# A convolution, router and low-rank experts on one core: tiles 2 and 3 in float32 with shared blocks, the first biases behind the sums, and another order of the early steps

## Chip, cores and metric

The kernel runs on one core of one Trainium2 chip. The metric is the device time of one execution in microseconds (us); the time of a kernel is the median of its runs.

## What is computed

The input x has 128 sequences of 32 channels and 512 positions. Cut to what matters:

```python
def reference(x, cond, conv_b, conv_w, cond_w, base_W, base_b, router_W, router_b, A, B, expert_map):
    c = conv1d(x, conv_w, taps=9, pad=4, groups=4) + (cond @ cond_w.T)[:, :, None] + conv_b[None, :, None]
    base = c @ base_W.T + base_b                          # 512 -> 512, along the positions
    probs = softmax(c @ router_W.T + router_b)            # 15 routes
    p, i = top_k(probs, 8)
    w = sum of p over the routes that expert_map sends to each of 8 experts
    h = (c @ A) * w                                       # 8 experts of rank 16: 128 columns
    return x + base + 2.0 * (h @ B)                       # all float32
```

## The kernel before, in words

A row is one sequence and channel. The 4096 rows are 32 tiles of 128; tile t holds group t % 4 of the convolution's channels for 16 sequences. The 512 positions are cut into 32 blocks of 16, so that a block of 8 channels by 16 positions fills the 128 partitions, and the convolution is a matmul with banded weights over blocks: an output block needs its own input block and a neighbour.

**Convolution.** The first four tiles (START = 4) are done in plain float32 by `conv_first` (L557 to L566): two matmuls a tile, 128x128 by 512 columns each (own block, neighbour), from `x_in`. From tile 4 on, `conv` (L568 to L593) works with less arithmetic: blocks are taken in pairs, the sum of weights meets one block (`S_SUM`), the own weights meet a difference of blocks (`S_OWN`), 256 columns each, and once for each two tiles a third product (`S_QUARTERS`, from `edges`) corrects both tiles' reaching halves in `edge_ps`. Each of these is three matmuls in the faster number format (float32r, written as high and low parts: high by high, low by high, high by low).

**Linear part.** The conditioned rows are transposed (`turn`, L861) into y and split into `y_hi` (ScalarE, `y_high` L396) and `y_lo` (GpSimd, `y_low` L501). `linear` (L598) multiplies them with `wide_hi` and `wide_lo` in four runs of the contraction: the front bank (128 columns of A, 16 of the router, half of the base: 400 columns) and the next bank (256 columns). `turn_hw` (L625) transposes the weighted h on TensorE, `up` (L637) adds h @ B onto the same banks in six matmuls of 256 columns.

**Order on TensorE** for tile t from 2 on (L757 to L770): wait for `out_added` of tile t - 2 (its bank is used again) and for `y_hi`; front bank of tile t (12 matmuls); `turn_hw` of tile t - 1; next bank, runs 0 and 1 (6); `up` of tile t - 1 (6); next bank, runs 2 and 3 (6); `conv` of tile t + 3 (6, or 9 when t + 3 is even). Tiles 0 and 1 have `first_step` (L678) and `second_step` (L712) of their own.

**Order on VectorE**, written out in `step` (L920 to L968): `condition` of tile t + 2 (L792: two adds of 256 columns, the second waiting for the first, then the 64-partition add from `edge_ps` at L809, which waits for the second), `turn` of t + 2 at once, `hw_low` (L873) of t - 1, `choose` (L819, adds the router's bias, starts when the front bank is done), `difference` of t + 4 (L813), `best` (L825), `add_out` of t - 1 (L776, adds the bank to the x rows), `mark` (L829), `weigh` (L834: five small operations, the last writes `hw`).

**ScalarE** (L430): `y_high`, `hw_high` (L403), `exponentials` (L365), `terms_high` (L381), `edge_high`, `odd_up` (L374, copies half of the terms into PSUM for `difference`). **GpSimd** (L519): `y_low`, `bias_rows` (L478, adds the base bias onto the x rows in `xr`, before `add_out` for every tile), `terms_low` (L483), `edge` or `edge_low`; in the start `conv_low` (L471) splits the convolution's weights. **SyncE** issues nearly all transfers, in the order of L273 to L300 and then of `step` (L302). Every operation signals a semaphore and each engine works its list in order: what waits holds up all behind it on that engine.

## Time and profile before

| | |
|---|---|
| median of 3 runs | 184.4 us (184.03 to 184.5) |
| the profiled execution | 184.55 us, its span 182.7 us |
| TensorE busy | 178.6 us, 98% of the span |
| VectorE busy | 150.9 us, 83% |
| GpSimd busy | 140.1 us, 77% |
| ScalarE busy | 81.3 us, 44% |
| granted TensorE clock | full (2.4 GHz) in all 40 slices |
| DMA | 32.01 MB, 175 GB/s over the span |
| chain that ended last | TensorE 97% |

The profiled execution's own time is 1.85 us more than its span, and 0.15 us above the median. TensorE's busy share counts pipelined matmuls, so it is read beside the chain and the waits.

### The profile page before, as it was taken

Reading aid. Unit: us, or ns where it says so; the run is one execution under the profiler, and the core shown is the slowest. Engines: PE = TensorE matmul, PEld = TensorE weight load, DVE = VectorE, ACT = ScalarE, POOL = GpSimd, SP = SyncE. Lnnn points to the kernel's source line nnn. Section 1 sums busy time; section 2 is a strip of 40 time slices with the busy share of each in tenths; the row PEclk is TensorE's granted clock in tenths of the full one; section 3 lists DMA queues with packets and bytes.
Section 4 is the critical chain, followed back from the end, with each engine's and each line's share of the span. In section 5 each row is a group of like instructions: output and inputs, shape, how many; then the busy total and the mean of one; then the engine's idle time right before and its main releaser. Section 6 shows DMA issues by size and latency. Waiting matters only on the chain.

```text
span 182.7 us, 3929 instructions
## 1 busy us (share of the span) xinstructions
PE 178.6 (98%) x1236; PEld 171.3 (94%) x1236; DVE 150.9 (83%) x509; ACT 81.3 (44%) x247; POOL 140.1 (77%) x139
## 2 busy tenths in 40 slices
PE   7999999999999999999999999999999999999993
PEld 3786999999999999999999999999999999999992
DVE  0597899888888889888888988889898889978673
ACT  3657834354544334454433445453344444422320
POOL 2127999999888898888889888888988887885610
PEclk9999999999999999999999999999999999999999
DMA  6999750766475653546475454745635721333304
GB/s 159 362 382 346 251 174 24 218 183 234 155 233 174 185 181 105 170 165 230 134 215 178 140 164 158 229 178 194 182 124 163 256 83 58 98 115 115 118 0 172
DMA packets 17876, 32.01 MB, mean 175 GB/s; under 512 B 1984, under 2 KB 3136, under 8 KB 17856
## 3 DMA queue, kind: packets, MB, share of 16 engines
q1 hardware_dynamic: 17424, 31.40, 52.7%
q10 hardware_dynamic: 432, 0.36, 0.6%
q8 instruction: 10, 0.16, 0.4%
q14 instruction: 10, 0.08, 0.2%
HBM read 23.36 MB, written 8.39 MB: 174 GB/s over the span
## 4 chain that ended last, share of the span: by engine, by line
PE 97%; DVE 1%; issue 0%; POOL 0%; DVEq 0%; POOLq 0%
PE wide_ps L605 61%; PE wide_ps L647 12%; PE conv_banks L591 11%; PE edge_bank L591 3%; PE conv_banks L605 2%; PE odd_bank L634 2%; PE wide_ps L553 1%; PE conv_banks L662 1%; PE conv_banks L564 1%; PE conv_banks L562 1%; DVE xr L978 1%; PE edge_bank L620 0%; PE conv_banks L647 0%; PE edge_bank L634 0%; POOL zeros L462 0%
## 5 line engine op out<-in xcount | busy, mean ns | idle before, releaser
L605 PE MATMUL wide_ps<-wide_hi,y_hi 128*128 128x400 f32 (+1 forms) x248 | 65.7, 325 | 0.0
L605 PE MATMUL wide_ps<-wide_lo,y_hi 128*128 128x400 f32 (+1 forms) x248 | 62.6, 313 | 0.0
L605 PE MATMUL wide_ps<-wide_hi,y_lo 128*128 128x400 f32 (+1 forms) x248 | 62.5, 312 | 0.0
L485 POOL TENSOR_TENSOR terms_lo<-terms,terms_hi 128x512 fp32r<-128x512 f32 x28 | 36.3, 1296 | 18.1 <-ACT terms_hi L385 18.0
L605 PEld LDWEIGHTS wide_ps<-wide_lo,y_hi 128*128 128x128 f32 x248 | 45.9, 188 | 0.2 <-DVE wide_lo L883 0.2
L605 PEld LDWEIGHTS wide_ps<-wide_hi,y_hi 128*128 128x128 f32 x248 | 43.9, 188 | 2.2 <-ACT y_hi L400 0.6
L605 PEld LDWEIGHTS wide_ps<-wide_hi,y_lo 128*128 128x128 f32 x248 | 45.8, 188 | 0.1
L503 POOL TENSOR_TENSOR y_lo<-y,y_hi 128x512 fp32r<-128x512 f32 x31 | 40.2, 1297 | 6.0 <-ACT y_hi L400 6.0
L480 POOL TENSOR_TENSOR xr<-xr,base_b_sb 128x512 f32<-128x512 f32 x32 | 41.5, 1300 | 0.0
L407 ACT ACTIVATE hw_hi<-odd_bank 128x128 fp32r<-128x128 f32 x31 | 8.6, 278 | 53.7 <-PE odd_bank L634 53.6
L780 DVE TENSOR_TENSOR xr<-wide_ps,xr 128x512 f32<-128x512 f32 x30 | 20.7, 691 | 5.2 <-PE wide_ps L647 3.6
L868 DVE STREAM_TRANSPOSE y<-y_rows 128x512 f32<-128x512 f32 x32 | 22.8, 711 | 1.1
L400 ACT ACTIVATE y_hi<-y 128x512 fp32r<-128x512 f32 x31 | 19.4, 624 | 3.8 <-DVE y L868 2.8
L367 ACT ACTIVATE minus_best<-top 128x1 f32<-128x1 f32 x32 | 6.5, 202 | 32.0 <-DVE top L827 32.0
L385 ACT ACTIVATE terms_hi<-terms 128x512 fp32r<-128x512 f32 x28 | 17.3, 618 | 0.5 <-DVE terms L816 0.5
L591 PE MATMUL conv_banks<-terms_hi,conv_hi 128*128 128x256 f32 x56 | 15.7, 280 | 0.0
L591 PE MATMUL conv_banks<-terms_hi,conv_lo 128*128 128x256 f32 x56 | 15.7, 280 | 0.0
L591 PE MATMUL conv_banks<-terms_lo,conv_hi 128*128 128x256 f32 x56 | 15.6, 278 | 0.0
L854 DVE SCALAR_TENSOR_TENSOR hw<-wide_ps,inv,expert_w 128x128 f32<-128x128 f32 x31 | 10.9, 351 | 4.9 <-DVE expert_w L848 0.5
L816 DVE TENSOR_TENSOR terms<-terms,odd_bank 128x256 f32<-128x256 f32 x28 | 11.7, 420 | 1.7 <-ACT odd_bank L379 0.8
L647 PE MATMUL wide_ps<-up_hi,hw_lo 128*128 128x256 f32 x62 | 12.7, 284 | 0.0
L806 DVE TENSOR_TENSOR y_rows<-conv_banks,y_rows 128x256 f32<-128x256 f32 x28 | 11.9, 425 | 1.0
(90 smaller groups left out, 308.9 us busy)
## 6 DMA issues: line engine op xcount, KB each, us to landing
xr<-x_rows SPq DMA_DIRECT2D x32, 256.0 KB, 3.6
out<-xr SPq DMA_DIRECT2D x31, 256.0 KB, 3.2
terms<-x_units SPq DMA_DIRECT2D x28, 256.0 KB, 2.9
edges<-x_edges SPq DMA_DIRECT2D x14, 256.0 KB, 3.1
wide_sb<-wide_w SPq DMA_DIRECT2D x4, 328.0 KB, 4.6
x_in<-x_first SPq DMA_DIRECT2D x3, 264.0 KB, 4.4
weights_sb<-conv_w SPq DMA_DIRECT2D x2, 192.0 KB, 5.3
x_in<-x_first SPq DMA_DIRECT2D x2, 132.0 KB, 2.8
```

Of the source, the lines that this page charges most:

```text
L385: nc.scalar.activation(terms_hi[i % 2][:, :, :, :], terms[i][:, :, :, :], ACT.Copy)\
L400: nc.scalar.activation(y_hi[k % 2][:, :, :], y[k % 2][:, :, :], ACT.Copy)\
L480: nc.gpsimd.tensor_tensor(xr[k][:, :], xr[k][:, :], base_b_sb[:, :], ALU.add)\
L485: nc.gpsimd.tensor_tensor(terms_lo[i % 2][:, :, :, :], terms[i][:, :, :, :], terms_hi[i % 2][:, :, :, :].bitcast(F32), ALU.subtract)\
L503: nc.gpsimd.tensor_tensor(y_lo[k % 2][:, :, :], y[k % 2][:, :, :], y_hi[k % 2][:, :, :].bitcast(F32), ALU.subtract)\
L591: mm = nc.tensor.matmul(sums, w[:, j, :], a[:, :, :], start=w is conv_hi and a is hi, stop=a is lo)
L605: mm = nc.tensor.matmul(sums_of(t, k)[:, b, 0:columns[1] - columns[0]], a[k % 2][:, r, :], w[:, r, columns[0]:columns[1]], start=r == 0 an ...
L647: mm = nc.tensor.matmul(sums_of(t, k)[:, b, first:first + HALF], a[k % 2][:, :], w[:, b * HALF:(b + 1) * HALF], start=False, stop=True, sk ...
L780: nc.vector.tensor_tensor(rows, linear_sums(t, k), rows, ALU.add)\
L806: nc.vector.tensor_tensor(rows[:, :, other, :], conv_ps[:, h, 1, :, :], rows[:, :, shared, :], ALU.add).then_inc(own_ready, 1)
L816: nc.vector.tensor_tensor(terms[i][:, 0, :, :], terms[i][:, 0, :, :], odd_ps, ALU.subtract).then_inc(differences_ready, 1)
L868: nc.vector.transpose(y[k % 2][:, :, :].rearrange("p r (n o) -> p n r o", n=Q), y_rows[k % 2][:, :, :, :].rearrange("p n a k -> p n (a k)"))\
```

## The change

Tiles 2 and 3 leave `conv_first` and are done with paired blocks too, but in plain float32 (`conv_whole`: two matmuls of 256 columns, and for tile 2 a third that serves both). Their differences of blocks are new operations: two on GpSimd before `conv_low(1)`, which wait for all of VectorE's `wide_low`, and one on VectorE before `weigh(0)`. Loads change with them; the weights have 12 blocks in place of 14, and the base bias comes as a full 128-row array in place of a broadcast of one row.

The bias of tiles 0 to 3 is added behind `add_out` instead of ahead of it; `bias_rows` of tiles 1 to 4 moves to later places of GpSimd's list. The stores of these tiles wait for it.

`condition` keeps its two adds; the third is `reach`, which comes after `best`. In every step from 4 on VectorE does `choose`, `best`, `reach`, `add_out`, `mark`, `difference`, `weigh` and then `turn`; steps 0 to 3 are written out. ScalarE does `y_high` behind `hw_high` (steps 2 and 3: behind `exponentials`). On TensorE the blocks of tile 4 are done in `second_step`, its edges in step 2.

```diff
+W_OWN, W_REACH, W_SUM, W_QUARTERS = (1, 2, 4, 7), (0, 3), (9, 10, 5, 8), (11, 6)
+W_ALL = 12
...
+first_terms = [sb(f"first_terms{i}", [P, 2, Q, MK]) for i in range(START - FIRST)]
+first_edges = sb("first_edges", [P, 2, Q, MK])
...
     load_conv(2)
-    load_x(2)
-    sync.wait_ge(wide_in[0], 16)
+    load_first_terms(0)
+    sync.wait_ge(wide_in[1], 16)
+    sync.dma_start(first_edges[:, :, :, :], x_edges[0]).then_inc(first_edges_in, 16)
+    load_conv(4)
+    sync.wait_ge(wide_in[2], 16)
     load_conv(3)
-    load_x(3)
-    sync.wait_ge(wide_in[2], 16)
+    load_first_terms(1)
+    sync.wait_ge(wide_in[3], 16)
     load_terms(START, 0)
     load_edges(START // 2, 0)
     sync.dma_start(up_sb[:, :], up_w).then_inc(up_in, 16)
-    sync.dma_start(base_b_sb[:, :], base_b.partition_broadcast(P)).then_inc(base_b_in, 16)
+    sync.dma_start(base_b_sb[:, :], base_b).then_inc(base_b_in, 16)
     sync.dma_start(xr[0][:, :], x_rows[0]).then_inc(xr_loaded[0], 16)
     load_terms(START + 1, 1)
-    sync.wait_ge(x_loaded[3], 16)
+    sync.wait_ge(first_terms_in[1], 16)
     sync.dma_start(xr[1][:, :], x_rows[1]).then_inc(xr_loaded[1], 16)
     load_terms(START + 2, 2)
     load_edges(START // 2 + 1, 1)
-    load_conv(4)
     load_terms(START + 3, 3)
...
-            sync.wait_ge(out_added, t - 1 if t < TILES else t)
+            if up_to_tile(t, POST + 1):
+                sync.wait_ge(xr_biased, t - 1)
+            else:
+                sync.wait_ge(out_added, t - 1 if t < TILES else t)
...
     y_high(1, 1, 2)
+    exponentials(0, 0)
     odd_up(START, 0)
-    exponentials(0, 0)
-    terms_high(START, 0)
     act.wait_ge(up_in, 16)
     nc.scalar.activation(up_hi[:, :], up_sb[:, :], ACT.Copy, scale=LORA_SCALE)\
         .then_inc(up_hi_ready, 1)
     nc.scalar.activation(up_scaled[:, :], up_sb[:, :], ACT.Copy, scale=LORA_SCALE)\
         .then_inc(up_scaled_ready, 1)
+    terms_high(START, 0)
     edge_high(START // 2, 0)
...
-        if up_to_tile(t, TILES - 2):
+        if from_tile(t, TILES - 3) and up_to_tile(t, TILES - 2):
             y_high(t + 1, k + 1)
...
         hw_high(t - 1, k - 1)
+        if t == 1:
+            act.wait_ge(hw_lo_ready, 1)
+            odd_up(START + 1, 1)
+        if t == 1 or from_tile(t, START) and up_to_tile(t, TILES - 4):
+            y_high(t + 1, k + 1)
         if up_to_tile(t, TILES - 2):
             exponentials(t, k)
-        if t == 1:
-            act.wait_ge(hw_lo_ready, 1)
-            odd_up(START + 1, 1)
+        if t == 2 or t == 3:
+            y_high(t + 1, k + 1)
...
+        if from_tile(t, POST):
+            pool.wait_ge(xr_loaded[k], (t - k) * 4 + 16)
+        else:
+            pool.wait_ge(out_added, t + 1)
         nc.gpsimd.tensor_tensor(xr[k][:, :], xr[k][:, :], base_b_sb[:, :], ALU.add)\
...
     conv_low(0)
+    pool.wait_ge(wide_lo_ready, RUNS)
+    pool.wait_ge(first_terms_in[0], 16)
+    nc.gpsimd.tensor_tensor(first_terms[0][:, 0, :, :], first_terms[0][:, 0, :, :],
+                            first_terms[0][:, 1, :, :], ALU.subtract)\
+        .then_inc(first_difference[0], 1)
+    pool.wait_ge(first_edges_in, 16)
+    nc.gpsimd.tensor_tensor(first_edges[:, 0, :, :], first_edges[:, 0, :, :],
+                            first_edges[:, 1, :, :], ALU.subtract)\
+        .then_inc(first_edge_ready, 1)
     conv_low(1)
     y_low(1, 1, 2)
...
         if t == 0:
+            up_low()
             terms_low(t + 4, k)
-            up_low()
             edge_low(p + 2, k // 2)
+            y_low(t + 2, k + 2)
             pool.wait_ge(base_b_in, 16)
-            bias_rows(t, k)
-            y_low(t + 2, k + 2)
+            bias_rows(0, 0)
             return
         if t == 1:
             terms_low(t + 4, k)
-            bias_rows(t, k)
             edge(p + 3, 1 - k // 2)
             y_low(t + 2, k + 2)
+            return
+        if t == 2:
+            terms_low(t + 4, k)
             conv_low(2)
+            edge_low(p + 2, k // 2)
             conv_low(3)
+            bias_rows(1, 1)
             return
-        if from_tile(t, 3) and up_to_tile(t, TILES - 2):
+        if up_to_tile(t, TILES - 2):
             y_low(t + 1, k + 1)
-        if up_to_tile(t, TILES - 1):
+        if from_tile(t, START + 1) and up_to_tile(t, TILES - 1):
             bias_rows(t, k)
...
+        if t == 3:
+            bias_rows(2, 2)
+        if t == 4:
+            bias_rows(3, 3)
+            bias_rows(4, 0)
...
+    def conv_blocks(t, g):
...
+    def products(sums, j, hi, lo):
+        for w, a in ((conv_hi, hi), (conv_lo, hi), (conv_hi, lo)):
+            mm = nc.tensor.matmul(sums, w[:, j, :], a[:, :, :],
+                                  start=w is conv_hi and a is hi, stop=a is lo)
+        return mm
...
+    def conv_blocks(t, g):
         h = g % 2
         pe.wait_ge(terms_lo_ready, t - START + 1)
...
+        pe.wait_ge(y_rows_ready, t - 1)
         if t < 2 * START and h == 0:
             pe.wait_ge(conv_lo_ready, 2 + g // 2 * 2)
...
+        products(conv_ps[:, h, 0, :, :], S_SUM[g], terms_hi[h][:, 1], terms_lo[h][:, 1])
+        return products(conv_ps[:, h, 1, :, :], S_OWN[g], terms_hi[h][:, 0],
+                        terms_lo[h][:, 0])
+    def conv_edges(t, g, p):
+        pe.wait_ge(y_rows_ready, t)
+        pe.wait_ge(edge_lo_ready, p - START // 2 + 1)
+        return products(edge_ps, S_QUARTERS[g // 2], edge_hi, edge_lo)
+    def conv(t, g, p):
+        mm = conv_blocks(t, g)
+        if g % 2 == 0:
+            mm = conv_edges(t, g, p)
         mm.then_inc(conv_done, 1)
...
             pe.wait_ge(odd_ready, 1)
+            pe.wait_ge(differences_ready, 1)
...
-    def conv_later(t):
+    def conv_whole(t):
+        i, h = t - FIRST, t % 2
         pe.wait_ge(y_rows_ready, t - 1)
-        pe.wait_ge(conv_w_in[2], 16)
-        pe.wait_ge(x_loaded[t], 16)
-        conv_first(t)
+        pe.wait_ge(conv_w_in[2 + i], 16)
+        pe.wait_ge(first_terms_in[i], 16)
+        nc.tensor.matmul(conv_ps[:, h, 0, :, :], conv_sb[:, W_SUM[t], :],
+                         first_terms[i][:, 1, :, :], start=True, stop=True)
+        pe.wait_ge(first_difference[i], 1)
+        mm = nc.tensor.matmul(conv_ps[:, h, 1, :, :], conv_sb[:, W_OWN[t], :],
+                              first_terms[i][:, 0, :, :], start=True, stop=True)
+        if h == 0:
+            pe.wait_ge(cond_biased, GROUPS)
+            pe.wait_ge(first_edge_ready, 1)
+            mm = nc.tensor.matmul(edge_ps, conv_sb[:, W_QUARTERS[t // 2], :],
+                                  first_edges[:, 0, :, :], start=True, stop=True)
+        mm.then_inc(conv_done, 1)
...
         y_rest(1)
+        w_rest(0)
         high(2)
         y_rest(2)
-        w_rest(0)
+        w_rest(1)
         high(3)
         linear(0, 0, (3,), products=(Y_REST,), last=(RUNS - 1, W_REST))
-        w_rest(1)
         w_rest(2)
...
-        conv_later(2)
+        conv_whole(2)
     def second_step():
         runs = range(RUNS)
         pe.wait_ge(y_hi_ready, 2)
         linear(1, 1, runs, (FRONT_BANK,), (HIGH,))
         linear(1, 1, runs, (FRONT_BANK,), (W_REST,))
+        conv_whole(3)
         pe.wait_ge(y_lo_ready, 2)
         linear(1, 1, runs, (FRONT_BANK,), (Y_REST,)).then_inc(front_done, 1)
-        conv_later(3)
         turn_hw(0, 0)
-        linear(1, 1, runs[:3], (NEXT_BANK,))
+        linear(1, 1, runs[:2], (NEXT_BANK,))
         up(0, 0)
-        linear(1, 1, runs[3:], (NEXT_BANK,)).then_inc(linear_done, 1)
+        linear(1, 1, runs[2:], (NEXT_BANK,)).then_inc(linear_done, 1)
+        conv_blocks(START, 0)
...
+            if t == 2:
+                conv_edges(START, 0, START // 2).then_inc(conv_done, 1)
             up(t - 1, k - 1)
...
-        if from_tile(t, 1) and up_to_tile(t, TILES - 4):
+        if from_tile(t, 2) and up_to_tile(t, TILES - 4):
             conv(t + 3, (k + 3) % GROUPS, p + 2)
...
-        dve.wait_ge(xr_biased, t + 1)
+        if from_tile(t, POST):
+            dve.wait_ge(xr_biased, t + 1)
+        else:
+            dve.wait_ge(xr_loaded[k], 16)
...
         dve.wait_ge(conv_done, t + 1)
         c = cond_sb[:, g, bass.ds(q * Q, Q)]
         nc.vector.tensor_tensor(rows[:, :, shared, :], conv_ps[:, h, 0, :, :],
                                 c.unsqueeze(2).to_broadcast([P, Q, MK]), ALU.add)\
             .then_inc(common_ready, 1)
-        dve.wait_ge(common_ready, t - START + 1)
+        dve.wait_ge(common_ready, t - FIRST + 1)
         nc.vector.tensor_tensor(rows[:, :, other, :], conv_ps[:, h, 1, :, :],
                                 rows[:, :, shared, :], ALU.add).then_inc(own_ready, 1)
-        dve.wait_ge(own_ready, t - START + 1)
...
+    def reach(t, g):
...
+        h = g % 2
+        shared = 1 - h
+        rows = y_rows[h]
+        reached = slice(EDGE, P) if h == 0 else slice(0, EDGE)
...
+        dve.wait_ge(own_ready, t - FIRST + 1)
         nc.vector.tensor_tensor(rows[reached, :, shared, :], edge_ps[reached],
                                 rows[reached, :, shared, :], ALU.add)\
             .then_inc(y_rows_ready, 1)
...
     best(0, 0)
-    difference(START, 0)
     dve.wait_ge(top_ready, 1)
     mark(0, 0)
+    dve.wait_ge(first_terms_in[1], 16)
+    nc.vector.tensor_tensor(first_terms[1][:, 0, :, :], first_terms[1][:, 0, :, :],
+                            first_terms[1][:, 1, :, :], ALU.subtract)\
+        .then_inc(first_difference[1], 1)
     dve.wait_ge(is_expert_ready, 1)
     weigh(0, 0)
+    difference(START, 0)
     dve.wait_ge(cond_biased, GROUPS)
...
         if t == 0:
-            condition_first(2)
+            condition(2, 2, 0)
+            hw_low(0, 0)
+            reach(2, 2)
             turn(2, 2)
             choose(1, 1)
             dve.wait_ge(logits_ready, 2)
             best(1, 1)
+            return
+        if t == 1:
+            add_out(0, 0)
             dve.wait_ge(top_ready, 2)
             mark(1, 1)
-            condition_first(3)
-            hw_low(0, 0)
+            difference(START + 1, 1)
+            weigh(1, 1)
+            condition(3, 3, 0)
+            reach(3, 3)
             return
-        if t == 1:
+        if t == 2:
+            hw_low(1, 1)
+            choose(2, 2)
+            dve.wait_ge(logits_ready, 3)
+            best(2, 2)
             turn(3, 3)
-            difference(START + 1, 1)
-            add_out(0, 0)
-            weigh(1, 1)
+            add_out(1, 1)
+            dve.wait_ge(top_ready, 3)
+            mark(2, 2)
+            difference(START + 2, 2)
+            weigh(2, 2)
+            condition(4, 0, 1)
+            reach(4, 0)
+            return
+        if t == 3:
+            condition(5, 1, 1)
+            hw_low(2, 2)
+            choose(3, 3)
+            dve.wait_ge(logits_ready, 4)
+            best(3, 3)
+            turn(4, 0)
+            reach(5, 1)
+            add_out(2, 2)
+            dve.wait_ge(top_ready, 4)
+            mark(3, 3)
+            difference(START + 3, 3)
+            weigh(3, 3)
+            turn(5, 1)
             return
         if up_to_tile(t, TILES - 3):
             condition(t + 2, (k + 2) % GROUPS, q + (k + 2) // GROUPS)
-            turn(t + 2, k + 2)
-            hw_low(t - 1, k - 1)
-        elif t == TILES - 2:
+        if up_to_tile(t, TILES - 2):
             hw_low(t - 1, k - 1)
...
-        if up_to_tile(t, TILES - 2):
-            choose(t, k)
-            dve.wait_ge(logits_ready, t + 1)
-            if up_to_tile(t, TILES - 5):
-                difference(t + 4, k)
-            best(t, k)
-            dve.wait_ge(top_ready, t + 1)
-            if up_to_tile(t, TILES - 3):
-                add_out(t - 1, (k - 1) % UNROLL)
-            mark(t, k)
-            weigh(t, k)
+        choose(t, k)
+        dve.wait_ge(logits_ready, t + 1)
+        best(t, k)
+        if up_to_tile(t, TILES - 3):
+            reach(t + 2, (k + 2) % GROUPS)
+            if from_tile(t, TILES - 4):
+                turn(t + 2, k + 2)
+        dve.wait_ge(top_ready, t + 1)
+        if up_to_tile(t, TILES - 3):
+            add_out(t - 1, (k - 1) % UNROLL)
+        mark(t, k)
+        if up_to_tile(t, TILES - 5):
+            difference(t + 4, k)
+        weigh(t, k)
+        if up_to_tile(t, TILES - 5):
+            turn(t + 2, k + 2)
```

In `first_step` the product with `wide_lo` of runs 0 and 1 is done one place earlier each. The last four steps keep `turn` behind `reach`, ahead of `add_out`.

## Rows read from the trace of the kernel before

**Rows 1.** The page: span and the engines' busy time and share

```profile
span 182.7 us, 3929 instructions
...
PE 178.6 (98%) x1236; PEld 171.3 (94%) x1236; DVE 150.9 (83%) x509; ACT 81.3 (44%) x247; POOL 140.1 (77%) x139
```

**Rows 2.** Waits of TensorE (PE) in the whole span: total, times, longest

```profile
PE wide_ps L553 <- POOL zeros L462: 1.0, 1, 1.0
```

**Rows 3.** The chain that ended last, in order: start us, us, what

```profile
6.23 0.43 PE conv_banks L662 x2
...
13.02 0.86 PE conv_banks L562 x2
```

**Rows 4.** Timeline of TensorE's weight loads: start us, us, instruction, idle before

```profile
14.53 0.67 PEld L605 LDWEIGHTS wide_ps<-wide_hi,y_hi 128*128 128x128 f32 x4 [0.61 <-ACT y_hi L400]
```

**Rows 5.** Timeline of ScalarE (ACT): start us, us, instruction, idle before

```profile
13.85 0.63 ACT L400 ACTIVATE y_hi<-y 128x512 fp32r<-128x512 f32 x1 [1.90 <-DVE y L868]
...
35.11 0.28 ACT L407 ACTIVATE hw_hi<-odd_bank 128x128 fp32r<-128x128 f32 x1 [2.05 <-PE odd_bank L634]
```

**Rows 6.** Timeline of TensorE's matmuls, tiles 1, 2, 4, starts of 6 and 29

```profile
16.09 0.90 PE L605 MATMUL wide_ps<-wide_hi,y_lo 128*128 128x400 f32 x4
...
18.54 0.27 PE L634 MATMUL odd_bank<-ident,hw 128*128 128x128 f32 x1
...
21.85 0.97 PE L605 MATMUL wide_ps<-wide_hi,y_hi 128*128 128x400 f32 x4
...
32.57 0.88 PE L605 MATMUL wide_ps<-wide_hi,y_hi 128*128 128x400 f32 x4
...
34.74 0.27 PE L634 MATMUL odd_bank<-ident,hw 128*128 128x128 f32 x1
...
35.56 0.40 PE L647 MATMUL wide_ps<-up_hi,hw_hi 128*128 128x256 f32 x2
...
43.19 0.90 PE L605 MATMUL wide_ps<-wide_hi,y_hi 128*128 128x400 f32 x4
...
165.24 0.89 PE L605 MATMUL wide_ps<-wide_hi,y_hi 128*128 128x400 f32 x4
```

**Rows 7.** Timeline of VectorE (DVE), start and the steps of tiles 4 and 5

```profile
9.31 3.09 DVE L883 TENSOR_TENSOR wide_lo<-wide_sb,wide_hi 128x656 fp32r<-128x656 f32 x4
...
21.08 0.69 DVE L780 TENSOR_TENSOR xr<-wide_ps,xr 128x512 f32<-128x512 f32 x1 [0.53 <-POOL xr L480]
...
35.83 0.42 DVE L816 TENSOR_TENSOR terms<-terms,odd_bank 128x256 f32<-128x256 f32 x1
36.17 0.17 DVE L827 MAX8 top<-logits 128x8 f32<-128x15 f32 x1
36.57 0.69 DVE L780 TENSOR_TENSOR xr<-wide_ps,xr 128x512 f32<-128x512 f32 x1 [0.24 <-PE wide_ps L647]
...
37.53 0.18 DVE L838 SCALAR_TENSOR_TENSOR wide_ps<-wide_ps,exps 128x15 f32<-128x15 f32 x1
...
38.75 0.41 DVE L802 TENSOR_TENSOR y_rows<-conv_banks,cond_sb 128x256 f32<-128x256 f32 x1
39.20 0.42 DVE L806 TENSOR_TENSOR y_rows<-conv_banks,y_rows 128x256 f32<-128x256 f32 x1
39.66 0.42 DVE L809 TENSOR_TENSOR y_rows<-edge_bank,y_rows 64x256 f32<-64x256 f32 x1
```

**Rows 8.** Timeline of GpSimd (POOL) in steps 4 and 5

```profile
37.01 1.30 POOL L480 TENSOR_TENSOR xr<-xr,base_b_sb 128x512 f32<-128x512 f32 x1
38.27 1.30 POOL L485 TENSOR_TENSOR terms_lo<-terms,terms_hi 128x512 fp32r<-128x512 f32 x1
39.50 0.75 POOL L497 TENSOR_TENSOR edge_lo<-edges,edge_hi 128x256 fp32r<-128x256 f32 x1
40.20 1.31 POOL L503 TENSOR_TENSOR y_lo<-y,y_hi 128x512 fp32r<-128x512 f32 x1
```

68 lines of the change are left out of this document (28 added, 40 removed).

## The prediction

> **What bounds the kernel.** I read the page first: TensorE ends the chain, and VectorE and GpSimd are at 83% and 77% of a span of 182.7 us [rows 1]. Then the waits of TensorE: it waited once, 1.0 us at the very start [rows 2]. So every microsecond behind it is matmul time, and only two things change the end: less matmul work, or a stall of TensorE where there is none now. Then the chain in order, for prices, and last the timelines of the four engines between 9 and 44 us, to see how early each operand is ready. I write F(t) for the moment the front bank of tile t is done (start of the hw transpose); before, F(1) = 18.54, F(4) = 34.74 [rows 6].
>
> **TensorE's work.** A float32 matmul of 256 columns takes 0.43 us in the chain, one of 512 columns 0.86 [rows 3] (the chain splits each into two passes). Tiles 2 and 3 now cost 4 x 0.86 = 3.44 us, afterwards 3 + 2 matmuls of 256 columns, 5 x 0.43 = 2.15. That removes 1.29 us. The other moves on TensorE (blocks and edges of tile 4, the order of `first_step`) keep the count of matmuls; the last `wide_lo` still gates tile 0: VectorE has it at 9.31 + 3.09 = 12.40 [rows 7].
>
> **Tile 2's share is not cashed.** Tile 2's convolution starts at about 12.86 (the chain books it 0.16 later [rows 3]). Its third product waits for two GpSimd subtractions which wait for `wide_low`: 12.44 + 2 x 0.72 = 13.9, priced by the same form, 0.75 [rows 8]. It would be over at 14.35. But tile 1's front bank needs `y_hi`, which ScalarE finishes at 13.85 + 0.63 = 14.48 [rows 5], and TensorE's loads already sat idle for it until 14.53 [rows 4]. Nothing ahead of it on VectorE or ScalarE changes, so tile 1 starts at 14.53 again: 0.43 us of the 1.29 become a wait, and the two subtractions are hidden by that same wait (without it they cost 0.2). GpSimd's `y_lo` of tile 1 is now late (16.2), which is why tile 3's convolution stands ahead of it.
>
> **Tile 3's share is.** The low product of tile 1 started at 16.09 [rows 6]; now two matmuls (0.86) come first, then 0.73: F(1) = 17.69, 0.85 earlier than 18.54. hw of tile 0 is ready at about 16.4: its `exponentials` go ahead of `odd_up` on ScalarE (-0.30), the new subtraction on VectorE (0.34) hides behind them. Transfers: some 300 KB more come ahead of tile 4's terms, under 1 us; each new landing that I sum stays 0.7 us or more ahead of its user, and the base bias no longer is read as a broadcast.
>
> **VectorE gets more work.** Before, tiles 2 and 3 took one add of 512 columns each; now three adds of 256, some 0.65 us more per tile, and 0.34 for the subtraction: about 1.6 us in a stretch where it had no more than 0.53 us idle at one place [rows 7]. Against it stands the new order. An add that waits for the add ahead of it starts 0.45 behind it (38.75, 39.20, 39.66), while a free one of 0.42 is followed after 0.34 (35.83 to 36.17) [rows 7]. Taking `reach` and `turn` away from the adds they wait for, and putting `difference` between `mark` and `weigh`, frees 0.11 + 0.10 + 0.14 + 0.18 = 0.53 us a tile; VectorE's list falls from 5.12 to about 4.6 us, under TensorE's 5.1 and 5.5 (two tiles from 32.57 to 43.19 are 10.62 [rows 6]). Followed step by step with these prices: `add_out(0)` ends at 20.57, tile 2 starts at 20.64 (was 21.85, with 0.35 us of tile 4's edges ahead of it, now behind: gain 0.86); the edges of tile 4 need `reach(3)`, 23.6, and come at 23.7; `hw_low(2)`, behind four adds and a fifth, is 0.1 us late for `up(2)`; tile 4 starts at 31.82 (was 32.57) and F(4) = 34.0. The gain there is 0.74.
>
> **GpSimd is late once, at tile 6.** The bias of tile 4 is still added ahead of `add_out(4)`, and step 4 puts it last: `y_low(5)`, `terms_low(8)`, `edge_low`, bias of tile 3, bias of tile 4. `terms_low(8)` waits for `terms_hi(8)`, this for `difference(8)`, this for `add_out(3)`, which waits for `up(3)`: F(4) + 1.83 (36.57 against 34.74 [rows 6, 7]). From there: `add_out` and `mark` 0.78 (0.96 from 36.57 to 37.53 [rows 7], less the 0.18 in which `weigh` waits for `mark`, and `difference` will not), `difference` 0.42, `terms_hi` 0.62 (the form of `y_hi`, 0.63) [rows 5, 7] with 0.1 of handing over: F(4) + 3.77. GpSimd then needs 1.25 + 0.70 + 1.25 + 1.30 = 4.50 (37.01 to 38.27, 39.50 to 40.20 [rows 8]), and the bias is there at F(4) + 8.27; `add_out(4)` takes 0.69 [rows 7]: F(4) + 9.0. TensorE wants to start tile 6, on that bank, two tiles after tile 4: its own work from F(4) is 43.19 - 34.74 = 8.45 [rows 6]. So it stands still for about 0.6 us. Bounds: if `terms_low(8)` never waited (GpSimd is free 0.4 us before), 0.15; if GpSimd were late by one more bias, 1.8. I take 0.6, since every price in the sum has its own row. The stores of tiles 0 to 3 now wait for the late biases, and on SyncE the loads of rows and terms stand behind them; followed through, each is still issued over 6 us ahead of its user. Of the gain of 0.74 about 0.1 is left, with a weight load exposed after the stall.
>
> **The steady part.** From step 5 on the same operations are in another order. Counted from F(t): `hw_hi` is ready at 0.65 (35.11 + 0.28 against 34.74 [rows 5, 6]), `hw_low` ends at 0.92 and is wanted at 1.29; `add_out` 1.83 to 2.52, wanted at 2.95 or 3.3; `weigh` takes 1.22 (37.53 to 38.75 [rows 7]), hw is ready at 4.3 and wanted at 5.1 or 5.5; `y_hi` at 1.2 and GpSimd's `y_lo` at 2.6, both wanted over 1.5 us later. None is late; in the last steps, with `turn` ahead of `add_out`, the bank is free 0.04 us before it is wanted, so up to 0.1 may be lost. From tile 6 to tile 29 TensorE took 165.24 - 43.19 = 122.05 us, 11.5 pairs of 10.61 [rows 6], all alike, so at most small delays sit in each. VectorE will reach `hw_low` and hw a little sooner than now. I count 0.2 us over all tiles as gained, a guess between 0 and 0.5 (0.04 a pair).
>
> **Sum.** 1.29 removed; 0.43 waits for `y_hi`, 0.1 late `hw_low`, 0.65 at tile 6 with its load, 0.2 gained later: -0.3 us. On the profiled execution, span 182.7 and 184.55 in all, this is 184.25; its time stands 0.15 over the median of 184.4, so I give 184.1.
>
> **Rivals.** A difference of 0.3% of this time, 0.55 us, is about what a measurement can tell from none.
>
> A (mine, 0.52): 184.1; its own range is 183.7 to 184.5.
>
> B, GpSimd is in time at tile 6 and the 0.75 stays: 184.4 - 0.75 - 0.2 = 183.45. For it: the margin of all of step 4 hangs on one chain, and 0.15 is its lower bound. Against: `terms_hi` was what GpSimd waited for in the old order too, and the new one makes it later. A larger gain in the steady part has the same effect. 0.30.
>
> C, slower: VectorE's starts do not move closer. Then its list stays 5.12 us a tile, the 1.6 us of new work is not absorbed, and the place is `hw_low` of tiles 2 to 4: I get 30.5 for `hw_low(2)` against 29.7 wanted, `add_out(2)` 0.2 behind tile 4's start, then 0.3 more at `up(3)`, and tile 6 starts 0.7 us later than before: 184.4 + 0.7 = 185.1. It decides from the point where `hw_low` ends later than F(t) + 1.29. Against: the 0.34 and 0.45 us in [rows 7]. The page "VectorE: DVE Perf Modes" of the Trainium skill, section "The DRAIN you can't avoid", says that the next operation starts only when the pipeline is empty and that a semaphore between two operations costs nothing extra; by that C is what should come, and these rows differ from it. 0.10.
>
> D: the change gains nothing because a wait that I price at 0 (the edges of tile 4, `out_added` for tile 2, the last steps) takes the rest: 184.4 and up to 184.9. 0.08.
>
> **Numbers.** 184.1 us. Range 183.3 to 184.9: it takes in B and D and leaves out C. Faster by over 0.3%: B and the lower edge of A, 0.36. Within: 0.52. Slower by over 0.3%: C and a little of D, 0.12.
>
> **What would show it.** Right: one wait of TensorE near 42.5 us for VectorE's `add_out`, itself waiting for GpSimd's bias, 0.5 to 0.7 us; F(1) near 17.7 with tile 1 still started at 14.5 behind `y_hi`; tile 4 started near 31.8; VectorE with idle time in every step. Wrong: no wait of TensorE at tile 6 (B); an add and a `reach` or `hw_low` behind it 0.45 apart, or waits of `up` for `hw_lo` (C); tile 1 started before 14.4, which would cash tile 2's share as well; waits of TensorE behind 50 us.

## The result, and the profile after

The changed kernel takes 186.53 us (186.22 to 186.96, 6 runs); the kernel before, run beside it, 184.45 (184.03 to 185.3). The ratio is 1.010, 95% interval 1.0075 to 1.0126: slower by 1.4 to 2.3 us, outside the predicted range of 183.3 to 184.9. The profiled execution took 186.76 us with a span of 184.9. One of the twelve runs of e9 below took 998 us and is left out; no other run stands apart like this.

The page, span and engines, beside [rows 1]:

```profile
span 184.9 us, 3931 instructions
...
PE 179.8 (97%) x1238; PEld 172.2 (93%) x1238; DVE 146.9 (79%) x514; ACT 83.2 (45%) x247; POOL 141.4 (76%) x141
```

The waits of TensorE over the whole span, beside [rows 2]:

```profile
PE wide_ps L598 <- POOL zeros L485: 1.0, 1, 1.0
PE wide_ps L653 <- DVE xr L852: 0.5, 1, 0.5
PE wide_ps L699 <- DVE hw_lo L954: 0.3, 1, 0.3
```

Two waits are new and together 0.8 us; the kernel lost about 2. So the waits don't tell the loss. What does is the moment at which TensorE starts the front bank of each tile. The timeline of TensorE, beside [rows 6] (start us, us, instruction; the starts of tiles 0, 1, 2, 4, 6, 7, 24, 28 and 29, the transposes that follow the front banks of tiles 1 and 4, and the late product of `up(2)`):

```profile
9.26 0.57 PE L653 MATMUL wide_ps<-wide_hi,y_hi 128*128 128x400 f32 x2
...
15.07 0.99 PE L653 MATMUL wide_ps<-wide_hi,y_hi 128*128 128x400 f32 x4
...
18.22 0.27 PE L684 MATMUL odd_bank<-ident,hw 128*128 128x128 f32 x1
...
21.40 0.99 PE L653 MATMUL wide_ps<-wide_hi,y_hi 128*128 128x400 f32 x4
...
30.94 0.50 PE L699 MATMUL wide_ps<-up_hi,hw_lo 128*128 128x256 f32 x2 [0.30 <-DVE hw_lo L954]
...
33.05 0.34 PE L653 MATMUL wide_ps<-wide_hi,y_hi 128*128 128x400 f32 x1
...
35.24 0.27 PE L684 MATMUL odd_bank<-ident,hw 128*128 128x128 f32 x1
...
44.30 0.45 PE L653 MATMUL wide_ps<-wide_hi,y_hi 128*128 128x400 f32 x1 [0.45 <-DVE xr L852]
...
49.55 0.34 PE L653 MATMUL wide_ps<-wide_hi,y_hi 128*128 128x400 f32 x1
...
140.19 0.35 PE L653 MATMUL wide_ps<-wide_hi,y_hi 128*128 128x400 f32 x1
...
161.75 0.34 PE L653 MATMUL wide_ps<-wide_hi,y_hi 128*128 128x400 f32 x1
...
167.19 0.45 PE L653 MATMUL wide_ps<-wide_hi,y_hi 128*128 128x400 f32 x1
```

From such rows of every profile comes this table. Each column is a stretch between two of these starts, in us; "end" runs from tile 29 to the end of the span, "sum" from the front bank of tile 0 to the end of the span. The span is given to 0.1 us, so the last two columns are good to 0.05. The experiments below are in it already, since they are read by it.

| kernel | tile 0 at | 0 to 4 | 4 to 7 | 7 to 24 | 24 to 28 | 28 to 29 | end | sum |
|---|---|---|---|---|---|---|---|---|
| before | 8.72 | 23.85 | 15.73 | 90.43 | 21.37 | 5.14 | 17.46 | 173.98 |
| before (e9) | 8.51 | 23.81 | 15.75 | 90.42 | 21.38 | 5.12 | 17.51 | 173.99 |
| after | 9.26 | 23.79 | 16.50 | 90.64 | 21.56 | 5.44 | 17.71 | 175.64 |
| e1, bias early | 9.53 | 23.80 | 15.81 | 90.61 | 21.56 | 5.44 | 17.75 | 174.97 |
| e5, order alone | 9.36 | 23.84 | 15.73 | 90.24 | 21.49 | 5.44 | 17.80 | 174.54 |
| e6, old order | 9.54 | 23.82 | 17.11 | 90.61 | 21.28 | 5.14 | 17.50 | 175.46 |
| e12, addresses | 9.08 | 23.80 | 16.47 | 90.31 | 21.48 | 5.44 | 17.72 | 175.22 |
| e13, three mended | 8.61 | 24.10 | 15.70 | 90.31 | 21.47 | 5.13 | 17.58 | 174.29 |

Behind tile 0 the changed kernel loses 1.66 us: nothing is won up to tile 4 (-0.06, forecast -0.75), 0.77 goes between tiles 4 and 7 (0.63 of it ahead of tile 6), 0.21 between tiles 7 and 24, 0.19 up to tile 28, 0.30 at tile 29, 0.25 in the end. The start adds 0.54 in this pair of profiles (last section).

### The profile page after: what moved, and what is told of

Same layout as the page of the kernel before. It is cut to its first block, busy times and chain, and to the rows that moved or that the text cites. A ratio compares the mean times of both kernels' runs of the same rounds, so it can differ in the third digit from the quotient of the medians.

```text
span 184.9 us, 3931 instructions
## 1 busy us (share of the span) xinstructions
PE 179.8 (97%) x1238; PEld 172.2 (93%) x1238; DVE 146.9 (79%) x514; ACT 83.2 (45%) x247; POOL 141.4 (76%) x141
## 3 DMA queue, kind: packets, MB, share of 16 engines
HBM read 23.48 MB, written 8.39 MB: 172 GB/s over the span
## 4 chain that ended last, share of the span: by engine, by line
PE 86%; DVE 7%; POOL 3%; issue 2%; ACT 1%; DVEq 0%; ACTq 0%; POOLq 0%
PE wide_ps L653 55%; PE wide_ps L699 10%; PE conv_banks L615 9%; PE edge_bank L615 2%; PE conv_banks L653 2%; DVE xr L852 2%; PE odd_bank L684 2%; PE conv_banks L714 2%; PE wide_ps L598 1%; POOL xr L506 1%; DVE y_rows L886 1%; DVE xr L1093 1%; POOL terms_lo L511 1%; DVE hw_lo L954 1%; PE conv_banks L733 1%
## 5 line engine op out<-in xcount | busy, mean ns | idle before, releaser
L954 DVE TENSOR_TENSOR hw_lo<-odd_bank,hw_hi 128x128 fp32r<-128x128 f32 x31 | 9.0, 291 | 11.5 <-ACT hw_hi L425 11.3
L875 DVE TENSOR_TENSOR y_rows<-conv_banks,y_rows 128x256 f32<-128x256 f32 x30 | 12.7, 425 | 1.0
L886 DVE TENSOR_TENSOR y_rows<-edge_bank,y_rows 64x256 f32<-64x256 f32 x30 | 12.4, 413 | 0.5
```

The source lines that it names most:

```text
L875: nc.vector.tensor_tensor(rows[:, :, other, :], conv_ps[:, h, 1, :, :], rows[:, :, shared, :], ALU.add).then_inc(own_ready, 1)
L886: nc.vector.tensor_tensor(rows[reached, :, shared, :], edge_ps[reached], rows[reached, :, shared, :], ALU.add)\
```

## The experiments

Fourteen runs: twelve variants and the kernel before twice more (e9, e10), each compared with runs of the kernel before on the same chip (medians there 184.46 to 184.76 us).

**e1: the bias of tile 4 early.**

```diff
@@ GpSimd, step
                     y_low(t + 1, k + 1)
+                if t == 4:
+                    bias_rows(4, 0)
...
                 if t == 4:
                     bias_rows(3, 3)
-                    bias_rows(4, 0)
```

(with a semaphore of its own, for which `add_out(4)` waits)

> The changed kernel, with the bias of tile 4 done by GpSimd in step 4 directly behind y_low(5), ahead of terms_low(8), on a semaphore of its own. Theory 1 (the loss is a sum of separate stalls of TensorE, this one the largest): add_out(4) no longer waits for the bias, tile 6 starts 8.45 us after the front bank of tile 4 in place of 9.06, and nothing later takes it back: 185.9 us against 186.5 for the changed kernel, ratio to the kernel before about 1.008. Theory 2 (VectorE's list as a whole is too long in steps 2 to 5): add_out(4) comes no more than 0.2 us earlier, or a later operand takes the gain: 186.3 to 186.5.

Measured: 185.92 us, ratio 1.0055 (1.0036 to 1.0075). In the changed kernel GpSimd (POOL) did this in step 4, and VectorE (DVE) waited for it:

```profile
38.98 1.29 POOL L511 TENSOR_TENSOR terms_lo<-terms,terms_hi 128x512 fp32r<-128x512 f32 x1 [0.59 <-ACT terms_hi L403]
40.23 0.74 POOL L523 TENSOR_TENSOR edge_lo<-edges,edge_hi 128x256 fp32r<-128x256 f32 x1
40.93 2.54 POOL L506 TENSOR_TENSOR xr<-xr,base_b_sb 128x512 f32<-128x512 f32 x2
...
43.56 0.69 DVE L852 TENSOR_TENSOR xr<-wide_ps,xr 128x512 f32<-128x512 f32 x1 [1.60 <-POOL xr L506]
```

The last line is `add_out(4)`; TensorE started tile 6 at 44.30. With the bias early the waits of TensorE are

```profile
PE wide_ps L600 <- POOL zeros L486: 1.0, 1, 1.0
PE wide_ps L701 <- DVE hw_lo L958: 0.3, 1, 0.3
```

and tile 6 starts 8.46 behind the transpose that ends tile 4 (35.53 to 43.99), against 9.06. The sum falls by 0.67. This part of the loss is shown.

**e2: `hw_low(2)` ahead of the condition of tile 5.**

```diff
@@ VectorE, step 3
-                    condition(5, 1, 1)
                     hw_low(2, 2)
+                    condition(5, 1, 1)
```

> The changed kernel, with hw_low(2) ahead of condition(5) in VectorE's step 3. Theory 1: the third product of up(2) waits no more, the next-bank matmuls behind it start 0.82 + 0.71 us after the front bank of tile 3 in place of 2.10, tile 4 starts about 0.5 us earlier and the wait at tile 6 stays as it is (9.06 behind the front bank of tile 4): 186.0 us. Theory 2: what follows on VectorE (turn(4), reach(5), add_out(2)) gates tile 4, so tile 4 starts at the same time: 186.5 us.

Measured: 186.57 us, 1.0095 (1.0058 to 1.0133). The wait of `up(2)` went, and smaller ones on the next operations of the same list took its place. Rows of VectorE (`reach(5)`, `add_out(2)`), then of TensorE (the next bank behind `up(2)`, the edge products, tile 4):

```profile
31.32 0.38 DVE L886 TENSOR_TENSOR y_rows<-edge_bank,y_rows 64x256 f32<-64x256 f32 x1
31.63 0.67 DVE L852 TENSOR_TENSOR xr<-wide_ps,xr 128x512 f32<-128x512 f32 x1
```

```profile
30.26 0.28 PE L653 MATMUL wide_ps<-wide_hi,y_hi 128*128 128x256 f32 x1
...
31.75 0.39 PE L615 MATMUL edge_bank<-edge_hi,conv_hi 128*128 128x256 f32 x1
...
32.35 0.45 PE L653 MATMUL wide_ps<-wide_hi,y_hi 128*128 128x400 f32 x1
```

The 15 matmuls from 30.26 to 32.35 took 2.09 us; at the 0.118 us from start to start that they have when nothing waits it would be 1.77. The 0.3 us between them are a late start behind `reach(5)`, a weight load exposed by it, and 0.13 us for `add_out(2)`. Tile 4 starts 23.73 behind tile 0, against 23.79. It is VectorE's list as a whole that gates tile 4, whichever of its operations TensorE meets first.

**e3: the turn behind `weigh` up to tile 28 as well.**

```diff
@@ VectorE, step
-                    if from_tile(t, TILES - 4):
+                    if from_tile(t, TILES - 3):
                         turn(t + 2, k + 2)
...
-                if up_to_tile(t, TILES - 5):
+                if up_to_tile(t, TILES - 4):
                     turn(t + 2, k + 2)
```

> The changed kernel, with turn(30) in step 28 behind weigh, as in all steps ahead of it, in place of ahead of add_out. Theory 1: tile 29 starts 5.14 us behind tile 28 in place of 5.44, and the rest of the end is the same: 186.2 us. Theory 2: the late turn makes y_hi of tile 30 late and the end loses as much: 186.5 us or more.

Measured: 186.53 us, 1.0082 (1.0053 to 1.0112); the stretch from tile 28 to 29 is 5.15 in place of 5.44, the sum 0.26 less. In the changed kernel VectorE had, ahead of tile 29 at 167.19:

```profile
165.24 0.43 DVE L886 TENSOR_TENSOR y_rows<-edge_bank,y_rows 64x256 f32<-64x256 f32 x1
165.70 0.71 DVE L945 STREAM_TRANSPOSE y<-y_rows 128x512 f32<-128x512 f32 x1
166.44 0.69 DVE L852 TENSOR_TENSOR xr<-wide_ps,xr 128x512 f32<-128x512 f32 x1
```

The 0.3 us are in the profile; the times of so few runs don't resolve them, and the expected 186.2 us was not met. The start of tile 30 behind tile 29 also falls, from 4.55 to 4.44 us (4.42 in the kernel before).

**e4: `reach` of even tiles on all 128 partitions.** It adds the edge sums to the lower 64 partitions too, so the conditioned rows of even tiles change and with them the output.

```diff
@@ VectorE, reach
-                reached = slice(EDGE, P) if h == 0 else slice(0, EDGE)
+                reached = slice(0, P) if h == 0 else slice(0, EDGE)
```

> The changed kernel, with reach of even tiles done on all 128 partitions from partition 0, in place of partitions 64 to 127; it adds edge sums to rows that should not have them. Same columns, so the same duration. Theory H (an operation of VectorE whose operands start at another partition than those of the operation ahead is held until that has ended): behind reach and behind the turn of even tiles the next start comes 0.64 and 0.35 us later in place of 0.75 and 0.46 to 0.54, hw_low(2) comes about 0.3 us earlier, tile 2 starts up to 0.2 us earlier: 186.0 us. Rival (the gaps are semaphore waits and not the partitions): starts and time as in the changed kernel, 186.5 us.

Measured: 185.94 us, 1.0054 (1.0024 to 1.0083). The timeline of VectorE ahead of tile 2, first of the changed kernel, then of e4 (start us, us):

```profile
19.16 0.43 DVE L886 TENSOR_TENSOR y_rows<-edge_bank,y_rows 64x256 f32<-64x256 f32 x1
19.62 0.71 DVE L945 STREAM_TRANSPOSE y<-y_rows 128x512 f32<-128x512 f32 x1
20.37 0.17 DVE L899 TENSOR_TENSOR logits<-wide_ps,weights_sb 128x15 f32<-128x15 f32 x1
```

```profile
19.06 0.41 DVE L886 TENSOR_TENSOR y_rows<-edge_bank,y_rows 128x256 f32<-128x256 f32 x1
19.51 0.71 DVE L945 STREAM_TRANSPOSE y<-y_rows 128x512 f32<-128x512 f32 x1
20.15 0.13 DVE L899 TENSOR_TENSOR logits<-wide_ps,weights_sb 128x15 f32<-128x15 f32 x1
```

The transpose of the same size is followed after 0.64 us in place of 0.75. `reach(2)` itself starts 0.20 behind `hw_low(0)` in place of 0.32, and what follows `reach(4)` 0.34 behind it in place of 0.46. Tile 2 starts 11.92 behind tile 0 (12.14 in the changed kernel), tile 4 23.39 (23.79). Twice the partitions, and faster.

The edit changes two things, the first partition (64 to 0) and the number of partitions (64 to 128). The trace of the kernel before tells them apart, for the `reach` of odd tiles has 64 partitions too, but from partition 0. The transpose of tile 4 with what follows it, then that of tile 5:

```profile
24.24 0.71 DVE L868 STREAM_TRANSPOSE y<-y_rows 128x512 f32<-128x512 f32 x1
24.99 0.29 DVE L877 TENSOR_TENSOR hw_lo<-odd_bank,hw_hi 128x128 fp32r<-128x128 f32 x1
...
29.52 0.71 DVE L868 STREAM_TRANSPOSE y<-y_rows 128x512 f32<-128x512 f32 x1
30.16 0.25 DVE L877 TENSOR_TENSOR hw_lo<-odd_bank,hw_hi 128x128 fp32r<-128x128 f32 x1
```

0.75 us behind the even tile, 0.64 behind the odd one: it is the first partition that costs. The sign of it stood in the trace of before.

At the end e4 has one more result: the stretch from tile 28 to 29 is 5.15 in place of 5.44, as in e3, although `turn(30)` still stands ahead of `add_out(28)` here. `reach(30)` starts 0.12 us sooner behind `best` there and `add_out` follows the transpose after 0.63 in place of 0.74.

**e5: the kernel before with the new order of VectorE and of `y_high` from step 4 on; e6: the changed kernel with the old one.**

```diff
@@ e5: the kernel before, VectorE, step (from t = START on)
                     choose(t, k)
                     dve.wait_ge(logits_ready, t + 1)
-                    if up_to_tile(t, TILES - 5):
-                        difference(t + 4, k)
                     best(t, k)
+                    if up_to_tile(t, TILES - 3):
+                        reach(t + 2, (k + 2) % GROUPS)
+                        if from_tile(t, TILES - 4):
+                            turn(t + 2, k + 2)
...
                     mark(t, k)
+                    if up_to_tile(t, TILES - 5):
+                        difference(t + 4, k)
                     weigh(t, k)
+                    if up_to_tile(t, TILES - 5):
+                        turn(t + 2, k + 2)
```

> The kernel before, with the new order of VectorE's list and of y_high on ScalarE from step 4 on only (the wait for the turned rows is put ahead of the edge products alone, as in the change); steps 0 to 3 stay as before. Theory P, the order costs: each pair of tiles 10.65 instead of 10.61 from tile 7 to tile 24 (+0.2 for the stretch), 0.3 more in tiles 24 to 28, tile 28's interval 5.4 instead of 5.14, the end 0.2 later: span 0.8 to 1.0 longer counted from the front bank of tile 0, time about 185.3. Rival Q, the prediction's term (the order gives 0 to 0.5 and loses up to 0.1): 184.0 to 184.6, the stretches as before. Rival R, the steady part's loss in the changed kernel comes from its start (the phase in which the engines enter tile 7): then the stretch from tile 7 to tile 24 is 90.43 as before and only tile 28 and the end lose, 184.9.

> The changed kernel with the old order of VectorE's list and of y_high from step 4 on. Theory P: tile 7 to tile 24 90.4, tiles 24 to 28 21.4 and tile 28's interval 5.15 as before, span 0.8 to 1.0 shorter counted from the front bank of tile 0, time about 185.7, and it differs from the changed kernel by as much as the new order alone does from the kernel before. Rival Q: 186.5, the stretches as in the changed kernel. Rival R: stretch from tile 7 to tile 24 stays 90.6, only the last tiles gain, 186.0.

Measured: e5 185.69 us, 1.0074 (1.0049 to 1.0098); e6 186.79, 1.0125 (1.0099 to 1.0151). Both times are above what any of the theories had; e5's sum is only 0.56 above that of the kernel before, and the rest of its 1.2 us is the start (last section). Two starts of TensorE in e5, tile 7 and tile 24:

```profile
48.93 0.89 PE L605 MATMUL wide_ps<-wide_hi,y_hi 128*128 128x400 f32 x4
...
139.17 0.90 PE L605 MATMUL wide_ps<-wide_hi,y_hi 128*128 128x400 f32 x4
```

That is 90.24 us against 90.43: in the long middle the new order gains 0.19, so theory P was wrong there, and the prediction's term was right. But it pays 0.30 at tile 29 and about 0.3 in the end, and once 0.28 at tile 26, for 0.56 in all. In e6 these losses are gone, the middle keeps its 90.61, and a new loss stands where the two orders meet: the end of step 3 turns tile 5's rows late, as the new order left them, step 4 turns tile 6's early, as the old one wants them, and `hw_low` comes behind both.

```profile
34.59 0.70 DVE L945 STREAM_TRANSPOSE y<-y_rows 128x512 f32<-128x512 f32 x1
...
36.56 0.71 DVE L945 STREAM_TRANSPOSE y<-y_rows 128x512 f32<-128x512 f32 x1
37.30 0.29 DVE L954 TENSOR_TENSOR hw_lo<-odd_bank,hw_hi 128x128 fp32r<-128x128 f32 x1
```

Tile 4 takes 6.04 us there in place of 5.13, and TensorE waits 0.6 for `hw_lo`. So putting back one half of a reordering is not the undoing of it.

**e7: a product of tile 3 into the wait for `y_hi(1)`.**

```diff
@@ TensorE, first_step
                 conv_whole(2)
+                conv_whole(3, 0)
...
-                conv_whole(3)
+                conv_whole(3, 1)
```

> The changed kernel with the first convolution product of tile 3 (0.43 us of TensorE) ahead of the front bank of tile 1, where TensorE waits 0.6 for y_hi(1). The prediction's term (0.43 of the 1.29 us taken out is given to this wait): the hw transpose of tile 1 starts 0.4 earlier, 8.5 to 8.6 behind the front bank of tile 0 instead of 8.96. Theory S, VectorE's list gates tile 2 and tile 4: tile 2's front bank moves by 0.2 at most and tile 4's by 0.1 at most, time 186.4 to 186.5. Rival T, TensorE's own chain gates them: tiles 2, 4 and 6 all 0.4 earlier, time 186.1.

Measured: 186.85 us, 1.0139 (1.0113 to 1.0164), and neither theory: tile 1's transpose came 0.28 later behind tile 0, not 0.4 earlier. The product's weight load could not start before its rows had landed:

```profile
14.72 0.30 PEld L731 LDWEIGHTS conv_banks<-first_terms,weights_sb 128*128 128x128 f32 x2 [0.48 <-issue]
```

VectorE's subtraction on the same transfer waited for it until 14.64. That profile began early (tile 0 at 8.64). In e8, which has the same edit and began at 9.37, the rows were there, the product started at 15.19, tile 1 6.07 behind tile 0 in place of 5.81, and its transpose 8.87 behind: 0.09 earlier, not 0.4. The wait that I wanted to fill was no longer there: in the changed kernel the third product of tile 2 starts at 14.58, a matmul of this form takes 0.43 [rows 3], and tile 1 starts at 15.07, right behind it.

**e8: bias early, `hw_low(2)` first, e7's product and the old order together** (the edits above).

> All that is known to help, together: bias of tile 4 early, hw_low(2) ahead of the condition of tile 5, the product of tile 3 in the wait of tile 1, the old order from step 4 on. If the gains add: 186.5 less 0.6 (bias) less 0.8 (old order) less 0 to 0.4 (product) less 0 to 0.3 (hw_low), 184.4 to 185.1, even with the kernel before. If VectorE's list in steps 1 to 3 still gates tile 4 (front bank of tile 4 23.5 or more behind that of tile 0, before 23.85): 185.0 to 185.3, slower than before only by what tiles 5 to 7 lose. If a start freed of these waits counts in full: 183.9, faster than the kernel before.

Measured: 186.31 us, 1.0104 (1.0077 to 1.0131), above all three forecasts. Tile 4 came 23.48 behind tile 0, 0.37 earlier than before, and tile 4 itself then took 6.36, the seam of e6. The gains did not add.

**e9 and e10: the kernel before, again.**

> The kernel before, unchanged, to see how its start varies: in the profiles taken so far the front bank of tile 0 starts at 8.62 to 9.53, 8.72 in the one profile of the kernel before. Theory V, the start varies by itself: its front bank of tile 0 is anywhere from 8.6 to 9.6, all stretches behind it as in the first profile within 0.1 (tile 0 to tile 4 23.85, to tile 7 39.58, tile 7 to tile 24 90.43). Rival W, the changed kernels start later by their own doing: 8.7 again, and 0.5 to 0.6 of the difference in time belongs to the start. Ratio 1.000 within 0.003 either way.

> The same kernel once more, for one more look at its start. Theory V: between 8.6 and 9.6, and another value than the last. Rival W: 8.7.

Measured: e9 184.53 us, 0.9994 (0.9969 to 1.0019), e10 184.6 in its one run; tile 0 at 8.51 and 8.95, sums 173.99 and 173.85. The sums repeat within 0.15, the start does not.

**e11: the edits of e1 and e3 together.**

> The changed kernel with its two measured waits taken away together: the bias of tile 4 early, and the turn late up to tile 28. If they add: counted from the front bank of tile 0 the span is 1.0 shorter than that of the changed kernel (0.7 and 0.3), 174.6 to 174.8, time about 185.6. If the second is hidden once the first is gone: 174.9 to 175.1, time 185.9 as with the first alone. Neither theory has it below the kernel before (173.98).

Measured: 185.43 us, 1.0034 (1.0012 to 1.0057), sum 174.62: they add.

**e12: the changed kernel with its SBUF tiles at the old addresses.**

```diff
@@ allocations
+        weights_pad = sb("weights_pad", [P, 2 * P])
...
-        first_edges = sb("first_edges", [P, 2, Q, MK])
+        terms_pad = sb("terms_pad", [P, 32])
...
         hw_lo = [sb(f"hw_lo{i}", [P, P], F32R) for i in range(2)]
+        first_edges = sb("first_edges", [P, 2, Q, MK])
```

> The changed kernel with every SBUF tile from the weights' pieces and the terms on at the address that it has in the kernel before (256 and 32 columns of padding, the first edges behind everything). Theory A, the 0.04 us by which a pair of tiles is slower in every changed kernel (10.64 against 10.60 with the same order in the kernel before) comes from where the tiles lie: tile 7 to tile 24 90.24 instead of 90.64. Rival B, it comes from something else: 90.64 stays, time 186.5.

Measured: 186.07 us, 1.0074 (1.0046 to 1.0102). No instruction differs, and tiles 7 and 24 start at

```profile
49.35 0.52 PE L655 MATMUL wide_ps<-wide_hi,y_hi 128*128 128x400 f32 x2
...
139.66 0.34 PE L655 MATMUL wide_ps<-wide_hi,y_hi 128*128 128x400 f32 x1
```

90.31 us apart in place of 90.64, and 10.58 in place of 10.64 from tile 26 to 28. Theory A held in this stretch (it had 90.24).

**e13: e1, e3 and e12 together; e14: e4's edit on top** (output changed as in e4).

> The changed kernel with the bias of tile 4 early, the turn late up to tile 28 and the tiles at the addresses of the kernel before. If the three add: span counted from the front bank of tile 0 175.64 - 0.7 - 0.3 - 0.4 = 174.2, against 173.98 of the kernel before: within 0.3 per cent of it, 184.7 to 185.1. If the address effect was another chance of the run: 174.6 and tile 7 to tile 24 90.6.

> The same with the reach of even tiles on all 128 partitions (the upper 64 partitions' addend is then added to the lower ones as well, so the output changes). If the held partitions keep the won time from tile 4: tile 4's front bank 23.4 behind that of tile 0 instead of 23.8, span 173.8 counted from it, 0.4 below e13, time 184.3 to 184.7. If something else is late there now: tile 4 at 23.8 and no gain.

Measured: e13 185.04 us, 1.0009 (0.9995 to 1.0022); e14 184.66, 0.9987 (0.9971 to 1.0003). Three mends bring the changed kernel back to the kernel before within 0.3%, and the middle is at 90.31 again. e14 is 0.38 us below e13 in time, as expected, but its profile doesn't show it: tile 4 is 24.56 behind tile 0, where 23.4 was expected. That profile and e13's began early (tile 0 at 8.24 and 8.61), and TensorE met a wait for `hw_hi` (0.4 and 0.6 us) that the others don't have. In e14 VectorE also waited 0.76 us for the rows of tile 3. A count from tile 0 is not fair to so early a start: what waits for a landing does not move with tile 0 (`up_hi` began at 16.34 in e13, at 16.24 in the changed kernel). ScalarE, then TensorE, in e13:

```profile
16.34 0.63 ACT L444 ACTIVATE up_hi<-up_sb 128x512 fp32r<-128x512 f32 x1 [1.21 <-DMA up_sb<-up_w]
...
18.23 0.25 ACT L428 ACTIVATE hw_hi<-odd_bank 128x128 fp32r<-128x128 f32 x1
```

```profile
18.62 0.48 PE L703 MATMUL wide_ps<-up_hi,hw_hi 128*128 128x256 f32 x2 [0.61 <-ACT hw_hi L428]
```

No version tried beats the kernel before by more than a measurement can tell.

## Why the prediction was wrong

**TensorE's work and tile 1: right, with no room left.** Tile 1 started 5.81 us behind tile 0 in both kernels, and the transpose behind its front bank came 8.96 behind tile 0 instead of 9.82, 0.86 earlier (forecast 0.85). The new third product of tile 2 was forecast to be over 0.13 us ahead of `y_hi`; it ended with it (14.58 + 0.43 = 15.01, `y_hi` was ready at 15.01, and tile 1 starts at 15.07). So the forecast wait of TensorE for `y_hi` was full of work and of the wait for GpSimd's subtractions. The new subtraction on VectorE was priced at 0.34 us and took 0.80 (1.19 in e14, 1.53 in e7), for which the profile names nothing; in the changed kernel this cost nothing, since VectorE waited 0.80 us for `hw_hi` later in its list.

**VectorE's list between tiles 2 and 4: the step that failed first.** The prediction had every operation that waits for nothing follow at the free distance, 0.34 us behind an add of 0.42, and tile 4 start 23.10 behind tile 0; it was 23.79. e4 shows 0.40 of the 0.69: a `reach` on partitions 64 to 127 that waits for nothing starts 0.12 us late, and the next operation that reads PSUM 0.11 or 0.12 us late, also with the transpose between them. In e4, without these, tile 2 starts 11.92 behind tile 0, as forecast. A further 0.2 is in the trace without an experiment of its own: VectorE stood still ahead of `weigh(2)` for nothing that the profile names, in every changed kernel. With this the list had no slack left: e2 took away one wait and TensorE met the next operation of the same list. The whole 0.86 won at tile 1 was gone by tile 4.

**Tile 6: the mechanism right, the cushion gone.** Tile 6 was forecast to start 9.0 behind the end of tile 4's front bank, and did at 9.06. The bias was ready 8.23 behind that point (forecast 8.27; the terms add up to 8.25). The stall was to eat a gain of 0.74; with no gain there it was a plain loss of 0.67 (e1).

**The steady part: the term right, the stretch wrong.** "I count 0.2 us over all tiles as gained" is what e5 measured, 0.19, at the addresses of before. It was a guess by its own words, so the agreement is in part luck. At the new addresses the order gains nothing (90.64 against 90.61 with the old one, e6). The changed kernel lost 0.21 in the middle, because its tiles lie at other addresses, which costs 0.33 (e12), plus some 0.08 in the tiles behind. Neither I nor anything in the trace of before priced where new tiles in SBUF push the old ones.

**The last steps: mis-sized.** "up to 0.1 may be lost" was 0.30 at tile 29. It takes both the `turn` ahead of `add_out` (gone in e3) and the late starts around a `reach` on partitions 64 to 127 (gone in e4); with either of the two gone the stretch is 5.15. So this is the wrong price of VectorE's list once more. The end loses 0.25: 0.13 between the starts of tiles 29 and 30, of which e3 gives back 0.11, and 0.12 between 30 and 31 (3.15 against 3.03), which comes with the new order (3.16 in e5, 3.02 in e6) and for which no run names the operation. Another 0.28 is lost at one tile, 26, in all eleven profiles with the new order there and in neither of the two changed kernels with the old one (e6, e8); it is the late start of ScalarE in the last section; the kernel before has 0.15 of its own a tile later, which the change does away with.

**Transfers said to be covered.** "each new landing that I sum stays 0.7 us or more ahead of its user" is wrong for `up_w`: ScalarE waited 0.43 us for it in the changed kernel (never in the kernel before) and 1.21 in e13. In most starts this costs nothing, since `hw_hi` then waits for TensorE; in the two earliest of the changed kernels, e14 and e13, it held TensorE for 0.4 and 0.6 us. It is wrong in an early start for the rows of tile 3 too (VectorE waited 0.42 in e7, 0.76 in e14).

**The rivals.** C was nearest in time (185.1) and right that some of VectorE's starts don't move closer, but wrong in why: free operations did start 0.34 apart, as [rows 7] say. Its page of the Trainium skill, "VectorE: DVE Perf Modes", section "The DRAIN you can't avoid", adds itself that an operation that is not held starts earlier, and points to the section "Two Vector instructions with no wait between them". There an operation is held, until all earlier ones of VectorE are finished, when an operand that it reads from SBUF or PSUM starts in another group of 32 partitions than the first operand that the last reader of that memory took from it, and likewise for what it writes. The traces agree: 0.75 against 0.64 us behind the transpose in e4, and the same two values for even and odd tiles in the kernel before. I had weighed the first of these sections and not the second.

**What adds up.** The forecast for all behind tile 0 was -0.3 us (0.75 gained up to tile 4, 0.65 lost at tile 6, 0.2 gained later), and 1.66 was measured. Of the 1.96 between them 0.69 lie up to tile 4, 0.12 up to tile 7, 0.41 up to tile 24 and 0.74 behind it. What the mends take away, from tile 0 on: tile 6 0.67 (e1), addresses 0.42 (e12), the turn 0.26 (e3); e13 leaves 0.31 over the kernel before: 0.25 up to tile 4, where its early start met the wait for `hw_hi`, and the rest is tile 26 and the end less what the middle gains. What stays open is the start.

## What to carry to other kernels

Before counting a gain at the head of a pipeline, add up the list of the engine that must keep pace, with every start priced by its own neighbours (partitions included): a gain passes only as far as the next list without slack. A forecast stall is absorbed only by a gain that is really there. And when a change allocates, pin the addresses of what was there, or compare kernels with the same addresses.
